# Four stages of a twelve-stage decoder re-ordered: value products behind the first queries, waits split, pairs finished two behind

## The reference

```
# first router (layer 0, feed-forward): 8 experts, the gates from three Sinkhorn rounds, two experts per token
scores = (x @ router_w + router_b) / max(temperature, 0.1); gates = sinkhorn(scores)
# "cosine" stage (layer 2, self-attention): linear attention with rotary position and relu features
q, k, v = split(x @ Wqkv.T + bqkv); q, k = rmsnorm(q), rmsnorm(k); q, k = rope(q), rope(k)   # the tables are cosines and sines
out = rmsnorm((relu(q) @ (relu(k).T @ [v, 1]) normalised) @ Wout.T + bout)
# wide attention (layer 2, cross-attention): 16 heads of 64
q = x @ Wq + bq; k = y @ Wk + bk; v = y @ Wv + bv
out = softmax(q @ k.T / 8 + mask) @ v @ Wo + bo
# 8-bit stage (layer 3, feed-forward)
h = relu(quant(x) @ quant(w1).T + b1); out = quant(h) @ quant(w2).T + b2
```

## Time and profile before

| | us |
|---|---|
| profiled execution | 1865.9 |
| its span | 1864.1 |
| median of three runs | 1865.18 |
| first router, start to its first logits' addition | 403.6 to 416.8 |
| cosine stage | 934.5 to 1035.5 |
| wide attention | 1036.4 to about 1392 |
| 8-bit stage | about 1820 to 1864.1 |

### The profile page before, as it was taken

One profiled execution on the slowest core, in us unless ns is written; L12 is line 12 of the kernel. 1 busy time (PEld: TensorE's weight loads), 2 busy tenths in 40 slices (PEclk: granted clock), 3 DMA queues, 4 the chain that ended last, 5 costly groups with the idle time before them and its releaser, 6 DMA issues. The chain is left out here.

```text
span 1864.1 us, 32306 instructions
## 1 busy us (share of the span) xinstructions
PE 1439.3 (77%) x11270; PEld 880.9 (47%) x11270; DVE 1219.5 (65%) x3991; ACT 920.7 (49%) x2002; POOL 337.8 (18%) x358
## 2 busy tenths in 40 slices
PE   5998978872865689995456799999983995778874
PEld 2555434441753444442234356666653884544432
DVE  7777368865347867777656477777665224668886
ACT  4555257651322345555612377777761442137656
POOL 3320012111534144300021000000002333302100
PEclk9999999985997879996567699999995997689996
DMA  3320014211661024300010000000003572003300
GB/s 125 53 53 2 1 18 58 36 35 46 166 132 27 12 59 69 59 12 19 1 58 1 12 7 7 7 11 9 1 1 105 162 205 78 23 18 55 49 2 23
DMA packets 60159, 84.53 MB, mean 45 GB/s; under 512 B 8352, under 2 KB 46496, under 8 KB 59488
## 3 DMA queue, kind: packets, MB, share of 16 engines
q1 hardware_dynamic: 55008, 72.24, 15.9%
q0 software_dynamic: 4992, 10.23, 2.8%
HBM read 51.18 MB, written 9.18 MB: 32 GB/s over the span
## 5 line engine op out<-in xcount | busy, mean ns | idle before, releaser
L704 DVE TENSOR_REDUCE maxs<-ps 128x4 f32<-128x1024 f32 x192 | 234.9, 1224 | 60.4 <-PE ps L1035 59.0
L863 ACT ACTIVATE L_xattn_probs<-ps 128x1024 f32<-128x1024 f32 x192 | 196.5, 1024 | 83.3 <-PE ps L1060 79.1
L3448 ACT ACTIVATE wide_pr<-wide_sc,wide_nm 128x256 f32<-128x256 f32 x256 | 127.0, 497 | 12.6 <-DVE wide_nm L3383 12.0
L1537 POOL DMA_INDIRECT moe_xs<-normed,moe_table x92 | 87.1, 947 | 158.1 <-PE ps L1567 72.9
L1035 PE MATMUL ps<-keys,L_xattn_qs 64*128 64x256 bf16 x768 | 75.4, 275 | 36.8 <-DVE maxs L704 33.3
L1076 PE MATMUL ps<-L_xattn_probs,values 128*32 128x256 f32 x1536 | 102.8, 385 | 0.0
L3353 DVE CUSTOM_DVE_ANT_0 wide_sc<-ps,wide_mask 128x256 f32<-128x256 f32 x256 | 93.3, 421 | 13.0 <-PE ps L3474 11.9
L3378 DVE COPY wide_prT<-ps 128x512 f32<-128x512 f32 x64 | 44.3, 692 | 85.4 <-PE ps L3487 85.3
L1966 DVE SCALAR_TENSOR_TENSOR moe_z_sb<-ps,moe_wt,moe_a_sb 128x256 f32<-128x256 f32 x46 | 22.3, 484 | 93.9 <-ACT moe_a_sb L1997 93.9
L1060 PE MATMUL ps<-L_xattn_qm,keys 64*128 64x256 bf16 x768 | 74.5, 272 | 7.1 <-ACT L_xattn_probs L863 6.7
L3393 DVE TENSOR_SCALAR wide_pr<-wide_pr,wide_inv 128x256 f32<-128x256 f32 x256 | 74.4, 350 | 2.6
(11 more groups left out here) (627 smaller groups left out, 3693.1 us busy)
## 6 DMA issues: line engine op xcount, KB each, us to landing
moe_wt<-in_packed_experts SPq DMA_DIRECT2D x23, 707.0 KB, 4.5
moe_wt<-in_packed_experts SPq DMA_DIRECT2D x23, 384.0 KB, 3.8
keys<-L_xattn_k_parts SPq DMA_DIRECT2D x108, 64.0 KB
L_xattn_qs<-L_xattn_q_parts SPq DMA_DIRECT2D x108, 64.0 KB
expert_out<-moe_y SPq DMA_DIRECT2D x46, 128.0 KB, 1.8
weights<-in_packed_L_xattn SPq DMA_DIRECT2D x2, 1316.0 KB, 7.4
keys<-L_attn_k_parts SPq DMA_DIRECT2D x36, 64.0 KB
L_attn_qs<-L_attn_q_parts SPq DMA_DIRECT2D x36, 64.0 KB
```

The costliest lines, as they stand in the source:

```text
L704: v.tensor_reduce(nm, ps[:, BANK_M:BANK_M + 2, :].rearrange("p j (t n) -> p j t n", t=2), AX.X, ALU.max, negate=True).then_inc(S("m_used"), 1)
L863: a.activation(probs[:, s % RING, :, :, :].rearrange("p j t n -> p j (t n)"), ps[:, BANK_P:BANK_P + 2, :], ACT.Exp, scale=HD ** -0.5)\
L1537: g.indirect_dma_start(self.xs[:, j % BUFS, h * P:(h + 1) * P], None, C.normed, bass.IndirectOffsetOnAxis(self.table[:, n:n + 1], 0))\
L3448: ins = a.activation(pr[:, s % 3, j, qt, :], sc[:, s % 2, j, qt, :], ACT.Exp, bias=nm[:, s % 2, n:n + 1], accum_out=sums[:, s % 2, n:n + 1])
```

## The change

In the first router the table is preloaded after `centre_and_copy` and no more before it. In the cosine stage the statistics of tiles 12 to 15 are made after the first pair's query rotation; a second semaphore, `kkv_split`, is raised as soon as the first bias row is split, and PE waits for that one ahead of the token tiles and for `biases_split` only ahead of the projection. In the 8-bit stage `hq` holds all four pairs, so that DVE's wait for PE goes, and ACT's evictions and DVE's additions come two pairs behind instead of one. In the wide attention the first sequence's four value products leave places -7 to -4 and BANK_B; they now stand at places -2, -1, 0 and 1, each behind that place's query and key projections, and in four banks (BANK_T, BANK_T + 1, BANK_V, BANK_V + 1) that are free until the first transposes and weighted sums. DVE adds their bias at places -1, 0, 1 and 1, after the rest of that place. The transposes of the first sequence no longer wait for its values.

```diff
@@ sinkhorn_moe, scalar @@
+                centre_and_copy(a, C, xn, hT, normed)
                 a.preload_act_table_set("natural_log_exp_and_others")
-                centre_and_copy(a, C, xn, hT, normed)
@@ relu_attention, vector @@
-                        drain(norm_steps(v, L, C, AHEAD, TILES))
+                        L.settle()
...
                          .then_inc(S("q_rotated"), 1)
+                    if m == 0:
+                        drain(norm_steps(v, L, C, AHEAD, TILES))
                     yield
@@ relu_attention, gpsimd @@
                 L.settle()
+                g.memset(kkv_rest[0:1, 0:1], 0.0).then_inc(C.sem("kkv_split"), 1)
                 split_rows(g, L, out_parts[:, :], out_middle[:, :], out_rest[:, :], w("proj_b")[0:96, :])
@@ relu_attention, tensor @@
                     if m < 2:
-                        pe.wait_ge(C.sem("biases_split"), 1)
+                        pe.wait_ge(C.sem("kkv_split"), 1)
                     token_tile(0)
...
+                    if m < 2:
+                        pe.wait_ge(C.sem("biases_split"), 1)
                     pe.matmul(ps[:, B + 3, :], pick[:, :], bcast(out_parts[:, :], 1, [96, PT, D]), start=True, stop=False)
@@ int8_ffn, vector (hq: [P, 2, FT, PAIR] becomes [P, PAIRS, FT, PAIR]) @@
                 for m in range(PAIRS):
-                    if m >= 2:
-                        v.wait_ge(S("down_ready"), m - 1)
...
-                    if m > 0:
-                        add(m - 1)
+                    if m > 1:
+                        add(m - 2)
+                add(PAIRS - 2)
                 add(PAIRS - 1)
@@ int8_ffn, scalar @@
-                    if m > 0:
-                        if m == 1:
+                    if m > 1:
+                        if m == 2:
                             a.wait_ge(S("bias_ready"), 2)
-                        evict(m - 1)
+                        evict(m - 2)
+                evict(PAIRS - 2)
                 evict(PAIRS - 1)
@@ wide_attention @@
+    FIRST_BANKS, FIRST_ADDS = (BANK_T, BANK_T + 1, BANK_V, BANK_V + 1), (-1, 0, 1, 1)
@@ wide_attention, vector @@
                     for n in range(4):
-                        m = p.job(n + 2, 1)
+                        if s == FIRST_ADDS[n]:
+                            v.wait_ge(S("v_proj"), n + 1)
+                            cols = slice((n % 2) * 512, (n % 2) * 512 + 512)
+                            v.tensor_tensor(V[:, 0, n // 2, cols], ps[:, FIRST_BANKS[n], :], w("bv")[:, cols], ALU.add)\
+                             .then_inc(S("v_ready"), 1)
+                    for n in range(4):
+                        m = p.job(n + 2, 1, 1)
@@ wide_attention, tensor @@
                 def turn(s):
-                    if s:
+                    if s == 0:
+                        pe.wait_ge(S("v_ready"), 2)
+                    else:
...
+                    if 0 <= p.tau + 2 < 4:
+                        n = p.tau + 2
+                        yield pe.matmul(ps[:, FIRST_BANKS[n], :], cT(0, (n // 2) * P, (n // 2 + 1) * P),
+                                        w("wv")[:, (n % 2) * 512:(n % 2 + 1) * 512], start=True, stop=True)\
+                            .then_inc(S("v_proj"), 1)
                     for n in range(4):
-                        m = p.job(n + 1, 1)
+                        m = p.job(n + 1, 1, 1)
...
                     m = p.job(5, 1)
                     if m is not None:
-                        pe.wait_ge(S("v_ready"), 4 * (m + 1))
+                        if m:
+                            pe.wait_ge(S("v_ready"), 4 * (m + 1))
```

More of the change, by code:

```diff
@@ L3080, in int8_ffn @@
         h = sb("h", [P, PAIRS, FT, PAIR])
-        hq = sb("hq", [P, 2, FT, PAIR], BF16)
+        hq = sb("hq", [P, PAIRS, FT, PAIR], BF16)
         xmax = sb("xmax", [P, PAIRS])
@@ L3163, in _ @@
                 for m in range(PAIRS):
-                    if m >= 2:
-                        v.wait_ge(S("down_ready"), m - 1)
                     L(v.tensor_scalar(h[:, m, 0, :], h[:, m, 0, :], s1i[:, 1:2], ROUND, ALU.mult, ALU.add))
-                    v.tensor_scalar(hq[:, m % 2, 0, :], h[:, m, 0, :], -ROUND, None, ALU.add).then_inc(S("hq_ready"), 1)
+                    v.tensor_scalar(hq[:, m, 0, :], h[:, m, 0, :], -ROUND, None, ALU.add).then_inc(S("hq_ready"), 1)
                     v.wait_ge(S("h_rounded"), m + 1)
-                    v.tensor_scalar(hq[:, m % 2, 1:FT, :], h[:, m, 1:FT, :], -ROUND, None, ALU.add).then_inc(S("hq_ready"), 1)
-                    if m > 0:
-                        add(m - 1)
+                    v.tensor_scalar(hq[:, m, 1:FT, :], h[:, m, 1:FT, :], -ROUND, None, ALU.add).then_inc(S("hq_ready"), 1)
+                    if m > 1:
+                        add(m - 2)
+                add(PAIRS - 2)
                 add(PAIRS - 1)
@@ L3267, in _ @@
                         pe.wait_ge(S("hq_ready"), 2 * m + (1 if f == 0 else 2))
-                        mm = pe.matmul(ps[:, m, :], wT[:, 1, tile(f)], hq[:, m % 2, f, :], start=f == 0, stop=f == FT - 1)
+                        mm = pe.matmul(ps[:, m, :], wT[:, 1, tile(f)], hq[:, m, f, :], start=f == 0, stop=f == FT - 1)
                     mm.then_inc(S("down_ready"), 1)
@@ L3524, in beside @@
                                 pe.wait_ge(S("added"), m - 2)
-                            elif m:
+                            else:
                                 pe.wait_ge(S("hT_ready"), m)
```

## The result

The changed kernel took 1841.85 us, the median of four executions (1838.75 to 1846.11), beside 1865.53 us of the kernel before (1864.02 to 1870.23): a ratio of 0.987, interval 0.9844 to 0.9897. The execution that was profiled is the longest of the four, 1846.11 us with a span of 1843.9, so stages have to be compared one by one and not by the spans alone.

What follows compares the result with a forecast made beforehand. Serial waits bound four places, TensorE's products carrying the wait in two fills; TensorE bounds the wide attention after its fill. 1.2 + 4.6 + 10.0 + 4.6 = 20.4 off 1865.9 gives 1845.5 us; range 1843 to 1853 (8 in 10).

Steps and rivals of the forecast that it cites:

- the four terms: Gains forecast: first router 1.2 us, cosine stage 4.6, wide attention 10.0, 8-bit stage 4.6; sum 20.4.
- the rival in which it appears ahead of the centring: First router: a table load still precedes the first centring, the 1.2 us go, 1846.7 us; no separate chance given.
- the prediction's 946.6: Cosine stage: time when the moved statistics end and the key rotation starts, instead of 951.17; gain 4.6 us.
- one-column products had kept the clock down: Cosine stage before: no gap from 943.03 to 951.13, yet no clock rise, with 1.71 us of one-column products in the middle.
- the wait at the fourth value product that was to give 1.4 us back: Wide attention: fourth value product adds 1.0 us, VectorE adds its bias before masking slot 2, so slot 3's scores wait.
- the slots' pitch: Wide attention's live slots: 5.13 us per slot, bounded by TensorE; a pitch above that would show the prediction wrong.
- Both rivals that need a late clock: Cosine and wide fills: late in one, 1847.9 or 1851.0 to 1853.0 us, chance 0.19; in both, 1853.7 or 1855.7, 0.09.
- the slower one: Wide attention: clock stays low in live slots, 4.3 us more per slot; with five slots 1875.2 us; chance 0.03.
- between 4.33 and 4.82: 8-bit stage: one turn removed saves 4.33 us; 4.82 for the last eviction if TensorE is at the upper clock.
- the end stay as far behind: 8-bit stage: last addition and store were to stay as far behind their eviction as before.
- gives back what came early: Sign of being wrong: a later stage loses the time gained earlier; no size given.
- The low end of 1843: Whole kernel: lower end of the range 1843 to 1849 (ends of the terms, 0.7 for the median), and of 1843 to 1853.

Runs made afterwards that it cites:

- wide_filler: Kernel before, old order kept, with one unread product behind each of the wide attention's first four value products: 1857.50 us, ratio 0.9971.
- after_again: The changed kernel run once more with no edit, against the kernel before: 1840.66 us, ratio 0.9868.
- int8_only: Kernel before with only the 8-bit stage's part of the change: 1861.08 us, ratio 0.9979.
- the other kernel: Kernel before with only the wide attention's part, plus three empty VectorE steps (0.6 us) at that stage's end: 1853.33 us, ratio 0.9945.

## Why the prediction was right or wrong

The mechanisms of the four terms held, and each term came within about 1 us of its size. What failed is that the sum puts nothing for stages that nobody touched; the last paragraphs of this section are on that.

**The first router: right.** 1.2 forecast, 1.27 measured from the stage's start to the logits, the same in all traces. The load took 1.28 us and lies in ScalarE's wait; the rival in which it appears ahead of the centring fell. Of the drain of some 1380 ns that the Trainium skill adds to the load (ScalarE: Activation LUTs, "What ACT_TABLE_LOAD costs") the traces show nothing: in its new place the load starts 0.02 us after the copy ahead of it (415.23 + 0.60, then 415.85), and the logits gained 1.27 us and not 2.6.

**The cosine stage: the mechanism right, the term too large.** The tiles started behind the query products, the clock rose among them, the moved statistics became what the key rotation waits for, and 12.02 us from the start is what the prediction's 946.6 means (946.6 - 934.54 = 12.06). What was wrong is the other end of the difference. I took 16.63 us of one execution as the old code's value, and argued from that execution that one-column products had kept the clock down; the same code in eight more traces reached its key rotation at 14.3 to 17.2 us, and in five of the nine the upper clock was granted over a part of that stretch (in three from the one-column products on, in two ahead of the tiles). The term is 15.7 - 12.02 = 3.7 us instead of 4.6. By the stage's whole length it is 100.7 - 96.2 = 4.5, which holds the clock's changes further back too, and the two runs of the part alone gave 3.4 ± 1.6; so the term was too large for the step that it described, and the kernel's time can't tell 3.7 from 4.6.

**The wide attention: right in all its steps, 1.0 us too small and at the end of its bounds.** 11.0 us against 10.0, of 9 to 11. The scores of slots 0 and 3 were forecast at 7.8 and 20.6 to 21.1 us from the start and came at 7.1 and 19.9. The queries of the second place were to start at 1043.1, 6.7 us from the start; they came at 6.15, since the first value product fits with less delay than the 1.1 us I gave it, and all that follows moved along. The clock rose within 1043 to 1044, about as taken; the wait at the fourth value product that was to give 1.4 us back is in the trace (2.06 us of idle VectorE ahead of its addition, 2.4 forecast), and the slots' pitch stayed 5.13. Both rivals that need a late clock fell, and with them the slower one: the clock rose 7.7 to 8.1 us after the stage's start in every trace of this code.

**The 8-bit stage: right, 0.6 us too small.** 5.2 us against 4.6, of 4.3 to 4.9. From the second maximum to the last eviction it is 16.44 us in before (1842.33 to 1858.77) and 11.49 in after (1827.50 to 1838.99), 4.95 less, where 4.6 was taken between 4.33 and 4.82. From that eviction to the last addition's end it is 2.22 us instead of 2.54, where the prediction had the end stay as far behind. Both fit the clock over the last turns; windows of before, then of after:

```profile
1850.00:1861.00 11.00, 6.54 (x23) 3.29 (x22) 5.83 (x10) 4.08 (x5) 0.00 (x0) 0.69 0.16 48
```

```profile
1833.00:1841.20 8.20, 6.27 (x29) 3.14 (x27) 6.48 (x11) 4.81 (x6) 0.00 (x0) 0.86 0.24 68
```

With one turn's waiting gone TensorE is busier and is granted more of the upper clock, 0.86 instead of 0.69. That this is the whole of the 0.6 us was not tried apart.

**What was missing: the stages behind.** This is the step that failed. The sum has four terms, and for the stages behind each part it puts nothing: of the first router it says "What follows is one serial chain, so all 1.2 us reach the end", the other three are added in the same way, and a later stage is named only among the signs of being wrong, as one "that gives back what came early". The second router's stage gave 2.6 us more instead. It took 158.4 to 159.9 us (mean 159.05) in the seven traces with before's end of the wide attention, wide_filler's among them, and 156.2 to 156.8 (mean 156.4) in all but one of those with the shorter one and no added delay: 2.6 us, or 2.1 with the exception counted. This follows from where the stage begins against the clock's fall, as the seventeen traces and the delay of 2.7 us show. The account in stages is 1.3 + 3.7 + 11.0 + 2.6 + 5.2 = 23.8 us, against 22.8 ± 1.7 measured; the forecast's own four terms, as measured, give 21.2, not far from its 20.4. The low end of 1843 had been made of those four terms' ends in one execution and 0.7 us for the median. It held neither a change of the clock's course in a stage that isn't touched, 2 to 3 us, nor the spread from execution to execution, of the same size. With either it would have reached to about 1840.

A stage behind can take as well. In `after`, `after_again`, `int8_only` and `wide_filler` the untouched front of the last two stages, up to the second maximum, took 186.0 to 186.2 us; in the thirteen other traces 183.8 to 184.0. The clock rose 9.3 to 9.7 us after that front's start in the four, and 3.0 to 4.0 us in the thirteen. The first 12 us of it, after and then before:

```profile
1641.29:1653.29 12.00, 10.90 (x32) 5.72 (x34) 2.50 (x4) 7.55 (x15) 2.91 (x3) 0.60 0.22 67
```

```profile
1658.37:1670.37 12.00, 10.57 (x42) 5.41 (x43) 3.45 (x6) 8.86 (x17) 2.91 (x3) 0.83 0.22 67
```

So in two of the four traces of after some 2.3 us were lost here; spread over the four this is 1.1 us, and 23.8 becomes 22.7. Four traces are too few for that average, so the close match to 22.8 is not evidence.

Luck had a part in how far the miss went: the execution that the prediction subtracted from, 1865.9, lay 1.6 us above the mean of 1864.3. From that mean the four terms as measured give 1843.1, just inside the range, and with the second router's 2.6 us 1840.5.

**What stays open.** In `after_again` the second router's stage took 160.25 us although the wide attention was short (352.69); the clock stayed low there until 51 us after its start. Its clock fell 0.22 us ahead of that stage's start, where the short ones had 0.18 or less and the other long ones 0.66 or more, so it stands at the border between the two forms; why that execution came out 0.04 us on the other side, and what sets the moments at which "flow" takes 112.4 or 118.8 us in kernels that don't touch it, these runs don't tell.

## What to carry to other kernels

A stage that begins or runs at TensorE's lower clock has no fixed length: read it from several executions, or from the same stage in other kernels' traces, before a difference is built on it, and measure from the stage's own start. In the sum for such a kernel, let the range hold the clock's course in each stage behind the change, to either side: here 2 to 3 us for one stage, twice what the first router's part was worth. At a stage's start order the products so that TensorE has no gap, since that brings the clock up: unread products alone gave 6.4 of the re-ordering's 11.0 us here; and when work is moved behind a critical step, look at what the next step waits for then: here it was the moved work.

## What the runs showed of the hardware

- A delay can be free. 2.7 us of pure waiting between two stages changed the kernel's time by -1.4 ± 2.5 us, because the next stage then had the upper clock for a stretch of its start; in the trace of the other kernel 0.6 us of waiting took this away again.
- Work that nobody needs can shorten a stage: the unread products of wide_filler took the wide attention from 363.80 to 357.41 us, the value products falling from 2.05 to 1.13 us within 5 us.
- Where in a stage the clock changes differs between executions of one program, and between kernels that have that stage's code in common: the old cosine code reached its key rotation anywhere from 14.3 to 17.2 us after the stage's start, an untouched stage took from 112.4 to 118.8 us, and the executions of one kernel spread from 1858.93 to 1872.53 us.
- In its new form the cosine stage's key rotation came at 12.01 to 12.04 us in all six traces, although the clock rose anywhere from 5.3 to 8.4 us after the stage's start: once a VectorE chain sets the time, the clock no longer shows in it.
- Some tenths of a us decide: with the clock's fall 0.18 us or less ahead of the second router's start that stage took 156.2 to 156.8 us, with 0.22 us and 0.66 to 1.22 us ahead 158.4 to 160.3.
